# Fourteen routing steps of VectorE, spread over every second head of two batches

## What is computed

```python
x = x + xattn(layernorm(x), ctx)        # softmax over 77 context rows and the row's own key
h = layernorm(x)                        # then the second layer:
qkv = (h @ W_qkv + b_qkv).reshape(B, S, 3, 16, 32)
attn = softmax(einsum('bqhd,bkhd->bhqk', q, k) / sqrt(32))
attn_out = einsum('bhqk,bkhd->bqhd', attn, v).reshape(B, S, D)
gate = softmax(h @ W_gate + b_gate)     # 8 experts
top_g, top_i = top_k(gate, 2)
combine = sum(one_hot(top_i, 8) * top_g[..., None], axis=2)
expert_out = einsum('bsd,edf->bsef', h, W_experts) + b_experts
moe_out = einsum('bsef,bse->bsf', expert_out, combine)
x = x + attn_out + moe_out
```

## Time and profile before

| | before |
|---|---|
| time, median of 3 runs | 1382.1 us (1381.03 to 1385.08) |
| the profiled execution | 1382.4 us, of which the span is 1380.8 |
| mean granted clock of TensorE | 0.974 |
| PE busy | 1280.6 us (93%), 7744 matmuls |
| DVE busy | 964.2 us (70%), 2143 instructions |
| ACT busy | 898.4 us (65%), 1880 instructions |
| POOL busy | 373.8 us (27%), 580 instructions |
| chain that ended last | PE 69%, DVE 8%, DMA 7%, issue 6%, ACT 4%, POOL 4% |

### The profile page before, as it was taken

One profiled execution on the slowest core, in us unless ns is written; L12 is line 12 of the kernel. 1 busy time (PEld: TensorE's weight loads), 2 busy tenths in 40 slices (PEclk: granted clock), 3 DMA queues, 4 the chain that ended last, 5 costly groups with the idle time before them and its releaser, 6 DMA issues.

```text
span 1380.8 us, 27412 instructions
## 1 busy us (share of the span) xinstructions
PE 1280.6 (93%) x7744; PEld 987.1 (71%) x7745; DVE 964.2 (70%) x2143; ACT 898.4 (65%) x1880; POOL 373.8 (27%) x580
## 2 busy tenths in 40 slices
PE   4998999999798899999999999999998877899997
PEld 4977888888675567677777677776775655788775
DVE  4256888888768888888888888888886762344332
ACT  4123444454438889999999999999996862334332
POOL 0002222222200011310213102130003355677775
PEclk9998999999999999999999999999999997999999
DMA  5005777777665347455674555745559768877774
GB/s 167 0 1 203 277 267 252 268 261 252 225 175 166 75 110 182 87 131 136 150 178 84 124 139 156 167 84 152 121 116 227 247 183 237 217 148 138 136 139 59
DMA packets 113709, 222.22 MB, mean 161 GB/s; under 512 B 28538, under 2 KB 36874, under 8 KB 111348
## 3 DMA queue, kind: packets, MB, share of 16 engines
q1 hardware_dynamic: 84528, 177.94, 42.6%
q0 software_dynamic: 26624, 42.04, 17.1%
q10 hardware_dynamic: 2499, 1.55, 0.5%
HBM read 89.20 MB, written 77.75 MB: 121 GB/s over the span
## 4 chain that ended last, share of the span: by engine, by line
PE 69%; DVE 8%; DMA 7%; issue 6%; ACT 4%; POOL 4%; POOLq 1%; another core or an unknown queue 0%; SPq 0%; DVEq 0%; ACTq 0%
PE banks L231 13%; PE banks L233 13%; PE banks L232 13%; PE banks L1211 8%; PE banks L1192 8%; PE banks L1170 7%; DMA out_dram<-plain,score_bias 5%; POOL out_dram L679 2%; DVE plain L1703 1%; ACT plain L893 1%; ACT banks L886 1%; POOL plain L673 1%; PE banks L1052 1%; DMA plain<-in_L_xattn_Wq_dram 1%; PE banks L1088 1%
## 5 line engine op out<-in xcount | busy, mean ns | idle before, releaser
L231 PE MATMUL banks<-parts 128*128 128x512 f32 (+6 forms) x1108 | 442.2, 399 | 42.4 <-DVE parts L1789 9.6
L233 PE MATMUL banks<-parts 128*128 128x512 f32 (+6 forms) x1108 | 422.7, 382 | 0.0
L232 PE MATMUL banks<-parts 128*128 128x512 f32 (+6 forms) x1108 | 422.2, 381 | 0.0
L1703 DVE TENSOR_REDUCE plain<-banks 128x1 f32<-128x512 f32 x512 | 339.9, 687 | 72.4 <-PE banks L1170 54.6
L886 ACT ACTIVATE banks<-banks,plain 128x512 f32<-128x512 f32 x512 | 345.5, 681 | 15.1 <-DVE plain L1703 14.8
L893 ACT ACTIVATE plain<-banks 128x1024 f32<-128x1024 f32 x256 | 266.3, 1040 | 45.3 <-PE banks L1192 39.8
L231 PEld LDWEIGHTS banks<-parts 128*128 128x128 f32 (+1 forms) x1108 | 213.6, 193 | 91.8 <-issue 30.9
L233 PEld LDWEIGHTS banks<-parts 128*128 128x128 f32 (+1 forms) x1108 | 212.6, 192 | 41.1
L232 PEld LDWEIGHTS banks<-parts 128*128 128x128 f32 (+1 forms) x1108 | 214.1, 193 | 30.4
L1170 PE MATMUL banks<-parts 96*128 96x512 f32 x512 | 181.4, 404 | 0.2 <-issue 0.2
L1192 PE MATMUL banks<-parts 104*128 104x512 f32 x512 | 174.8, 422 | 1.2 <-ACT plain L893 1.2
(11 more groups left out here) (190 smaller groups left out, 1526.9 us busy)
## 6 DMA issues: line engine op xcount, KB each, us to landing
parts<-parts SPq DMA_DIRECT2D x384, 128.0 KB
parts<-h_turned SPq DMA_DIRECT2D x46, 512.0 KB, 6.1
experts_split<-parts SPq DMA_DIRECT2D x32, 512.0 KB, 4.1
h_turned<-parts SPq DMA_DIRECT2D x32, 512.0 KB, 2.9
parts<-experts_split SPq DMA_DIRECT2D x8, 2048.0 KB, 11.7
plain<-in_x_dram SPq DMA_DIRECT2D x32, 256.0 KB, 4.2
plain<-in_L_ffn_W_experts_dram SPq DMA_DIRECT2D x32, 256.0 KB, 4.2
out_dram<-plain SPq DMA_DIRECT2D x32, 256.0 KB, 2.8
```

What stands on the lines that cost most here:

```text
L231: pe.matmul(out, stat[0], mov[0], start=first, stop=False)
L232: pe.matmul(out, stat[0], mov[1], start=False, stop=False)
L233: return pe.matmul(out, stat[1], mov[0], start=False, stop=last)
L1703: dve.tensor_reduce(nmx[:, k, t:t + 1], bank[SB[t]][:], AX.X, ALU.max, negate=True).then_inc(q["f_max"], 1)
```

## The change

The fourteen functions behind the prefix sum now run behind every second head: behind heads 0, 2, ..., 14 of batch 0 and heads 0, 2, ..., 10 of batch 1 (head number `b * NH + k`). For this, batch 1 is written out on VectorE, and on SyncE too, so that SyncE's wait for `r_zero` comes behind batch 1. On GpSimd the three outputs that are due by then stand ahead of the wait, four `place` follow, and the loop covers batches 2 to 5. TensorE and ScalarE are as before. On VectorE the loop over batches 2 to 6 is made to begin at a multiple of 256 instructions (`addr_align`; with `max_nops=0` the padding is branched over).

```diff
@@ sync @@
             batch(0, True, False)
+            batch(1, False, False)
             sp.wait_ge(q["r_zero"], 1)
             sp.dma_start(slot_dram.rearrange("(p i) c -> p i c", p=P), lst).then_inc(q["r_zeroed"], 16)
-            with sp.Fori(1, B - 1) as b:
+            with sp.Fori(2, B - 1) as b:
                 batch(b, False, False)
             batch(B - 1, False, True)
@@ gpsimd @@
             attended(0, 0)
+            attended(0, 1)
+            attended(1, 0)
 
             pool.wait_ge(q["r_zero"], 1)
...
-            PER = (2 * B - 1) // (B - 3)
-            assert 1 + PER * (B - 3) == 2 * B
-            place(0)
-            attended(0, 1)
-            with pool.Fori(1, B - 2) as b:
-                place(PER * b - PER + 1)
+            PER = 3
+            AHEAD = 2 * B - PER * (B - 4)
+            assert AHEAD > 0
+            for m in range(AHEAD):
+                place(m)
+            attended(1, 1)
+            with pool.Fori(2, B - 2) as b:
+                place(PER * b + AHEAD - 2 * PER)
                 attended(b, 0)
                 for m in range(1, PER):
-                    place(PER * b - PER + 1 + m)
+                    place(PER * b + AHEAD - 2 * PER + m)
                 attended(b, 1)
@@ vector @@
-            LATER = {0: over_tiles_1, 1: over_tiles_2, 2: over_tiles_3, 3: first_blocks_1, 4: first_blocks_2, 5: rank_places, 6: places, 7: first_records,
-                     8: second_records, 10: block_experts, 11: block_places, 12: block_firsts, 13: block_order, 14: list_zero}
+            LATER = {2 * n: step for n, step in enumerate((
+                over_tiles_1, over_tiles_2, over_tiles_3, first_blocks_1, first_blocks_2, rank_places, places, first_records,
+                second_records, block_experts, block_places, block_firsts, block_order, list_zero))}
...
-                    if first and k in LATER:
-                        LATER[k]()
+                    if isinstance(b, int) and b * NH + k in LATER:
+                        LATER[b * NH + k]()
...
             batch(0, True, False)
-            with dve.Fori(1, B - 1) as b:
+            batch(1, False, False)
+            dve.addr_align(256, offset=0, max_nops=0)
+            with dve.Fori(2, B - 1) as b:
                 batch(b, False, False)
```

## The result

The changed kernel takes 1387.27 us (median of 13 runs, 1385.23 to 1391.34); the kernel before took 1381.03 in the 13 runs beside them. The ratio is 1.0048, with a 95% interval of 1.0034 to 1.0062: slower by 4.7 to 8.6 us. The forecast was 5.4 us slower. The profiled execution took 1387.13 us, 4.7 more than that of before.

The account below looks back on a forecast made before the run. TensorE, 99% busy, was taken as the bound. Waits 13.9, unseen time 3.5 and clock 1.7 sum to 19.1 us against 13.7: 5.4 more, 1387.8 profiled, median 1387.5; range for 8 in 10, 1378 to 1393.

Parts of the forecast that it names:

- Waits and margins: TensorE's waits for VectorE's split maxima behind routing steps, each step's length less its place's margin: 13.9 us against 9.7.
- "whole" heads: Heads 0, 4, 8, 12, behind which TensorE asks for the maxima first of all: margin taken as 0.25 us.
- "both" ones: Heads 2, 6, 10, 14, behind which TensorE asks for the maxima fourth: margin taken as 0.5 us.
- "ended" heads: Heads 3, 7, 11, 15, where TensorE asks for the maxima fifth, behind three score matmuls: margin 1.45 us, no longer used.
- Time that no wait shows: TensorE issue time lost beyond the visible waits: 0.29 us for each of twelve waits, 3.5 us against 2.3.
- The clock: TensorE at half speed behind the longest wait, in batch 1: one fall, 1.7 us against 1.7, bounds -1.7 and +1.7.
- Written-out code: Batch 1 written out on VectorE and SyncE, constants for register sums: gives nothing, bound 0 to -0.4 us.
- The aligned loop: VectorE's branch over padding ahead of batch 2: taken as 0, bounds 0 and 3.3 us.
- The rival of a broken loop: VectorE's loop fetches two blocks anew each pass, up to 3.3 us each, five passes: 33 us, 1415; chance 0.05.
- SyncE and GpSimd: SyncE's list wait moves behind batch 1's stack copies; GpSimd's `attended(1, 1)` goes out near 633, some 29 us to spare: cost 0.
- VectorE's idle time takes the steps: A step costs only what exceeds VectorE's 1.76 us idle over two heads: 10.9 us less, 1371 us; chance 0.17.
- The cancelling rival: Margin 0.5 behind "whole" too, nothing unseen per added wait, no clock fall: +1.0 us, 1383; chance 0.2.

Follow-up runs that it names:

- one entry later: Changed kernel with each step behind the split of the maxima of the next head instead of ahead of it: 1385.58 us, ratio 1.0033.
- old places in the new structure: Changed kernel with the fourteen steps back behind heads 0 to 8 and 10 to 14 of batch 0, batch 1 still written out, loop aligned: 1381.96 us, ratio 1.0002.
- dealt out over places with margins: Changed kernel with the 53 routing instructions issued one to five at a time behind the split in whole, begun and both lists: 1370.25 us, ratio 0.9918.
- shifted by 100: Kernel with dealt-out instructions, VectorE's program shifted once at its start (offset 100), loop not aligned right ahead of it: 1370.13 us, ratio 0.9910.
- steps at list starts: Changed kernel with each step behind the split of the maxima in the list of the next even head, two heads later: 1376.17 us, ratio 0.9964.
- behind "ended": Changed kernel with steps ahead of the split, only behind heads 3, 7, 11, 15 of batch 0 and 3, 7, 11 of batch 1: 1382.66 us, ratio 1.0011.
- not aligned: Changed kernel without the alignment of VectorE's loop: 1405.95 us, ratio 1.0167.

## Why the prediction was right

**Waits and margins.** Forecast 13.9 us, measured 13.7 (11 waits of 0.2 us or more). By place the margins were 0.11 to 0.19 behind "whole" heads (0.25 taken) and 0.26 to 0.60 behind "both" ones (0.5 taken). The largest error is a step that cost nothing: 1.26 us behind head 2 of batch 0, forecast at 0.76, has no wait of 0.2 us. These errors cancel, which is luck. The margin behind "ended" heads, on which the sign of the forecast hung, was tested by itself: 1.45 less than the steps' lengths.

**Time that no wait shows.** 0.29 us for each wait, 3.5 us in all, was too much. Batch 0 from head 2 lost 81.56 - 74.82 = 6.74 us with 5.6 us of waits, and batch 1 lost 97.87 - 85.17 = 12.7 against its length without steps, with 8.1 of waits and 3.4 of clock: together some 2.3 us.

**The clock.** One fall was forecast, at 1.7 us; it was one, but 6.80 us long: 3.4 us. That was the upper bound named. Its place and time were right. Its length could not be told from the wait: in the kernel with each step one entry later a wait of 2.88 us went with a fall of only 3.4 us.

**Batch by batch.** Batch 0 from head 2: 83 forecast, 81.6 measured. Batch 1: 97 and 97.9.

**Written-out code.** Bound at 0 to -0.4. Batch 1 became 0.8 us shorter (old places in the new structure). About half of that is ScalarE's wait for a stack copy, which left batch 1; the rest is at the bound.

**The aligned loop.** Taken as 0, it cost: batch 2 is 1.2 to 1.8 us longer than before in the five kernels in which VectorE stalls at the branch (in two of them with a wait of up to 0.6 us for a stack copy in it). The step that failed is the sentence that the stall would fall behind an "ended" head with 1.45 us of margin: the gap was 2.39 us of VectorE's time, longer than the margin. The bounds of 0 and 3.3 held. The rival of a broken loop did not come about, but only thanks to the alignment: without it the loop took 3.5 to 5.3 us more in each of the four passes that follow a back edge. The rival counted five such passes, of up to 6.6 us.

**SyncE and GpSimd.** 0 forecast, 0 measured for the wait that was named: nothing waits for `attended(1, 1)`. ScalarE's wait for a stack copy was not foreseen. In the changed kernel it is gone from batch 1 and does not come back in batch 2; in five of the seven other versions batch 2 has it, at 0.26 to 1.22 us.

**The rivals.** That VectorE's idle time takes the steps (1371) was wrong for these places, since batch 1 alone lost 12 us. It is not wrong of the engine: dealt out over places with margins, the same instructions cost 0.7 us in batch 1 (85.89 against 85.17 without steps), and that kernel takes 1370. Its idle time was there; the change did not reach it. The cancelling rival missed the waits by little and the clock by all; that nothing unseen is added per wait was right.

**The sum.** The waits (13.7), the time that no wait shows (2.3) and the clock (3.4) come to 19.4 us against the forecast's 19.1, since 1.2 too much for the second made up for most of the 1.7 too little for the third. With the 1.56 of batch 2 and the 0.8 of batch 1 the three batches lose 6.5 us, where 5.4 were forecast. The direction rests on a tested mechanism. That the total came so near is in part luck.

The profiled executions differ by 4.7 us, of which the first stage gave 0.9 back, batches 0 to 2 added 6.5, batches 3 to 6 and 7 gave back 0.3 and 2.4, and the third stage added 1.8. The last three were not forecast and have not been explained.

## What to carry over

Where an engine is not the bound, ask of each gap in its order who reads next what stands behind it, and how late that may be; insert work by that margin, not evenly. Spreading work over more places costs more if each place has less margin. Check every reader of the engine's next results, not only the first: moving the steps past one reader uncovered the next one. And when code grows ahead of a long loop, look at how long its passes take: the same loop, unchanged, cost 3.5 to 5.3 us more in each pass from one start and nothing from three others.

## What the runs showed of the hardware

- A loop of 266 recorded instructions on VectorE ran without a stall at its back edge from three starts (before, aligned, shifted by 100). From a fourth, VectorE stood still in two gaps, of 2.0 to 2.6 us and of 1.7 to 1.8 us, in each pass behind a back edge, and the pass took 89 to 91 us instead of 85.5. In that kernel 51 packets went through the instruction queue, against 32.
- A taken branch over padding went with a gap of 2.0 to 2.7 us on VectorE in five kernels, and with none in the one with nine more records ahead of it.
- TensorE's clock fell to 1.2 GHz for 3.4 us at single waits of 1.90 us (steps at list starts), 1.94 and 2.88 (one entry later), 2.14 (before, and old places), 2.32 (behind "ended") and 2.98 and 2.40 (not aligned). It fell for 6.8 us at 3.44 (after) and at 2.31 and 2.45 (not aligned). It did not fall at 2.15 and 2.00 us (behind "ended"). So the length of a single wait decided neither whether it fell nor for how long.
